# A reordered prologue, feature rows issued two a slot, and auxiliary work kept to slots 1 to 3 of every four

## The chip, the cores and the metric

The kernel runs on one core of one Trainium2 chip. The metric is the time of one execution on the device in microseconds (us), median of several runs. TensorE is called PE here, VectorE DVE, ScalarE ACT, GpSimd POOL and SyncE SP.

## What is computed

One layer on 1024 rows of 256 numbers: `x + attention(layernorm(x)) + ffn(layernorm(x))`. Attention has 16 heads of 16 numbers and two softmaxes over the same causal scores, one of them with a term from 8 "splat" features a head. The feed-forward part sends each row to the 2 best of 16 experts (at most 128 rows each) and to one shared expert.

```python
scores = einsum('bhid,bhjd->bhij', q, k) / sqrt(hd)
std_out = out_proj(softmax(where(mask, scores, neg)))
splat_attn = einsum(amp_b * qg, kg) + strength * einsum(amp_b * qg * qd, kg * kd)
gsa_out = out_proj(softmax(where(mask, scores + sensitivity * splat_attn, neg)))
attn = (1 - blend) * std_out + blend * gsa_out
...
h = silu(buf @ W1.T) * (buf @ W3.T)          # per expert, 128 rows of buf
y = sum over the 2 chosen experts of w * (h @ W2.T)
shared = (silu(xn @ Ws1.T) * (xn @ Ws3.T)) @ Ws2.T
```

## The kernel before

**Prologue.** The rows are normalized and transposed (`xnT`), and projected to q and k (`proj`). Exponentials and tanh of further products are the splat features (`feat`), `v` is projected, and the router's scores are made (`gate`). Each of these is an entry of the list `PRO`, which PE works off in order over five PSUM banks. q, k and the two feature tensors, each in two halves (eight items in `SPLIT_ORDER`), are written as three bf16 parts: `part0` and `part1` on ACT, the remainders by `rest_of` on DVE, and the third part by `third_of`, on DVE for items 0 to 3 and on POOL for items 4 to 7 (`POOL_THIRDS`). From these parts in `split`, SP's queue gathers the operand rows of each group into `stage`: 12 rows of q and k (`load_qk_row`, three buffers) and 19 of features (`load_feature_row`, two buffers). The last feature row comes from `gap_scratch`.

**Row maxima.** The softmax subtracts a row maximum, which rides as two extra rows of the q operand. The tasks `max2` and `max` make the scores of a row tile on PE and reduce them on DVE (`mx`); `max0` has the 6 tasks of the first query chunk of 512 rows, `max1` the 16 of the second. `shift` turns the result, negated and split in two, into a row (`mhl`, then `mT`), which SP writes to `stage` (`shift_rows`). In the prologue this is done for group 0, inside each group for the group after it.

**Groups.** There are 8 groups of two heads. A group walks over 6 pairs of key tiles, two pairs of the first query chunk and four of the second. One pair takes four slots, so a group has 24. On PE a pair is: the product of probabilities and v of the pair before (`pv`), slot 0, the splat scores of one key tile (`splat`), slot 1, `splat` of the other, slot 2, the plain scores of the next pair's first tile (`std`), slot 3, `std` of the second. ACT takes the exponential after each `std` and `splat`. In the slots stand auxiliary tasks by the table `PLAN`: the maxima and shifts, the output transposes `oT`, the routing steps `route` (on DVE, group 0), the shared expert in groups 0 and 1 (`sgu`, `shT`, `sy`), four experts in each of groups 2 to 5 (`xT`, `gu`, `hT`, `y`), and at the end `add`, `rows` and `out`. They share three PSUM banks in turn: a task waits on PE until DVE has emptied the bank of the third task before it (`aux_free`). For `gu` and `sgu` ACT makes a tanh behind its exponential of the same slot.

**SP's queue** walks over the same slots. At a `y` it waits until DVE has emptied it, writes it out and fetches the weights of the third expert after it; at a `shift` it waits for `mT`. One feature row of the next group is issued in each of slots 2 to 20, and one q or k row of the group after that in each of slots 0 to 11. PE waits for all 19 feature rows (`f_in`) before the first `splat` of a group.

## Time and profile before

| | us |
|---|---|
| runs | 407.89, 400.78, 406.73; median 406.73 |
| profiled execution | 399.62 |
| its span, first to last instruction | 397.8 |
| PE busy | 331.2 |
| DVE busy | 234.1 |
| ACT busy | 192.7 |

The profile is of one execution, and 1.8 us of its time lie outside the span. Busy times of the engines overlap. A group boundary is read from the copy `pv_sb<-ps` of a group's second chunk on DVE.

### The profile page before, as it was taken

The page shows a single profiled execution, that of the slowest core. Times are in us where ns is not written, and L with a number is a line of the kernel's source. Part 1 is how long each engine was busy: PE and PEld are TensorE (multiplying, and loading weights), DVE is VectorE, ACT ScalarE, POOL GpSimd, SP SyncE. Part 2 cuts the span into 40 slices and gives each one's busy share as a digit, 9 for nine tenths or more (in the row PEclk, how much of TensorE's full clock was granted, in tenths as well). Part 3 has the DMA queues.
Part 4 walks back from the last instruction along what each step waited for, and adds up shares of the span by engine and source line. Part 5 has one row for each costly group of instructions (what it writes and reads, how often), then busy time and mean ns, then how long its engine had stood idle before and what let it go on. Part 6 is the DMA issues. An engine that isn't in the chain of part 4 may idle for free.

```text
span 397.8 us, 6179 instructions
## 1 busy us (share of the span) xinstructions
PE 331.2 (83%) x2172; PEld 170.9 (43%) x2172; DVE 234.1 (59%) x613; ACT 192.7 (48%) x277; POOL 66.2 (17%) x82
## 2 busy tenths in 40 slices
PE   0999198588978999899978987999979999989974
PEld 0643075244434444444444443554535445434442
DVE  4566745768764754566446654584657646865322
ACT  1798721444534454445533553354445536857630
POOL 6200530000017630000000000010000004720000
PEclk9999777579999999999999999899999999999995
DMA  6328433050434333445543554346453333540011
GB/s 214 118 27 103 77 40 54 1 78 3 58 66 98 48 63 46 105 114 127 127 98 82 142 151 98 54 115 135 114 125 107 63 48 89 130 91 0 2 54 53
DMA packets 27330, 33.01 MB, mean 83 GB/s; under 512 B 6593, under 2 KB 20097, under 8 KB 27297
## 3 DMA queue, kind: packets, MB, share of 16 engines
q1 hardware_dynamic: 23745, 28.32, 34.1%
q0 software_dynamic: 2128, 4.22, 3.8%
q8 instruction: 19, 0.31, 0.3%
q10 hardware_dynamic: 1424, 0.04, 0.2%
q14 instruction: 14, 0.11, 0.1%
HBM read 15.60 MB, written 4.28 MB: 50 GB/s over the span
## 4 chain that ended last, share of the span: by engine, by line
PE 67%; DVE 15%; ACT 9%; DMA 4%; issue 3%; SPq 1%; DVEq 0%; ACTq 0%
PE ps L791 16%; PE ps L719 8%; PE ps L762 7%; ACT arena_p L610 6%; DVE mx L1065 6%; PE ps L692 5%; PE ps L774 5%; PE ps L728 5%; PE ps L650 3%; DMA stage<-gap_scratch 2%; PE ps L747 2%; PE ps L669 2%; PE ps L732 2%; PE ps L765 1%; PE ps L709 1%
## 5 line engine op out<-in xcount | busy, mean ns | idle before, releaser
L610 ACT ACTIVATE arena_p<-ps 128x1024 f32<-128x1024 f32 (+1 forms) x192 | 145.8, 811 | 87.8 <-PE ps L774 63.6
L1065 DVE TENSOR_REDUCE mx<-ps 128x1 f32<-128x512 f32 (+3 forms) x160 | 91.7, 591 | 60.7 <-PE ps L694 44.8
L791 PE MATMUL ps<-arena_p,v_full 128*32 128x512 f32 (+3 forms) x768 | 71.9, 492 | 0.6 <-ACT arena_p L610 0.6
L692 PE MATMUL ps<-stage 96*128 96x512 bf16 (+3 forms) x160 | 56.6, 369 | 8.3 <-DVE mx L1061 4.1
L762 PE MATMUL ps<-stage 98*128 98x512 bf16 (+1 forms) x192 | 50.9, 332 | 7.7 <-ACT arena_p L610 7.0
L774 PE MATMUL ps<-stage 98*128 98x512 bf16 (+1 forms) x192 | 46.5, 332 | 12.3 <-DMA stage<-gap_scratch 7.0
L615 ACT ACTIVATE small<-ps 128x176 f32<-128x176 f32 x24 | 7.6, 317 | 67.2 <-PE ps L719 67.2
L370 POOL DMA_INDIRECT wt<-xn_scratch,ids_sb x16 | 15.2, 949 | 146.3 <-PE ps L709 141.6
L791 PEld LDWEIGHTS ps<-arena_p,v_full 128*32 128x32 f32 x768 | 20.1, 109 | 34.3 <-issue 29.1
L692 PEld LDWEIGHTS ps<-stage 96*128 96x128 bf16 x160 | 15.6, 99 | 44.5 <-issue 24.8
L728 PE MATMUL ps<-arena_o,small 88*128 88x256 f32 x96 | 26.0, 393 | 5.4 <-DVE small L1088 5.3
L762 PEld LDWEIGHTS ps<-stage 98*128 98x128 bf16 x192 | 18.3, 99 | 27.2 <-ACT arena_p L610 15.9
L774 PEld LDWEIGHTS ps<-stage 98*128 98x128 bf16 x192 | 16.7, 98 | 28.2 <-ACT arena_p L610 8.9
L378 POOL DMA_INDIRECT ids_scratch<-tok,sidx x16 | 15.5, 966 | 68.6 <-DVE sidx L1019 64.1
L765 PE MATMUL ps<-mask_t,ident_b 128*128 128x128 bf16 x128 | 26.1, 223 | 0.0
L719 PE MATMUL ps<-w_sb,wt 128*128 128x352 f32 x64 | 23.5, 491 | 0.4
L694 PE MATMUL ps<-mask_n,ident_b 128*128 128x128 bf16 x96 | 22.3, 233 | 0.0
L728 PEld LDWEIGHTS ps<-arena_o,small 88*128 88x128 f32 x96 | 16.6, 190 | 10.4 <-DVE small L1088 8.1
L400 POOL DMA_INDIRECT xx<-ye_scratch,gidx x16 | 15.5, 968 | 32.9 <-issue 32.9
L1116 DVE COPY pv_sb<-ps 128x512 f32<-128x512 f32 x16 | 11.0, 690 | 16.1 <-PE ps L791 15.6
L1084 DVE SCALAR_TENSOR_TENSOR small<-small,ps 128x176 f32<-128x176 f32 x24 | 8.1, 338 | 21.0 <-ACT small L615 21.0
L885 DVE TENSOR_TENSOR acc<-ps,acc 128x256 f32<-128x256 f32 (+1 forms) x14 | 7.5, 538 | 17.1 <-PE ps L747 13.3
(189 smaller groups left out, 418.5 us busy)
## 6 DMA issues: line engine op xcount, KB each, us to landing
w_sb<-in_w_dram SPq DMA_DIRECT2D x16, 352.0 KB
stage<-split SPq DMA_DIRECT2D x48, 96.0 KB
stage<-split SPq DMA_DIRECT2D x48, 64.0 KB
arena_o<-in_w_dram SPq DMA_DIRECT2D x16, 176.0 KB
stage<-split SPq DMA_DIRECT2D x80, 32.0 KB
ye_scratch<-wt SPq DMA_DIRECT2D x16, 128.0 KB, 2.3
stage<-split SPq DMA_DIRECT2D x32, 48.0 KB
acc<-in_x_dram SPq DMA_DIRECT2D x2, 512.0 KB, 4.6
```

What stands on the lines that cost most here:

```text
L378: nc.gpsimd.indirect_dma_start(out=ids_d[:, :], out_offset=bass.IndirectOffsetOnAxis(ap=sidx[:, k, n:n + 1], axis=0), in_=tok[:, n:n + 1], ...
L400: nc.gpsimd.indirect_dma_start(out=gath[:, k, n, :], out_offset=None, in_=ye_d[:, :], in_offset=bass.IndirectOffsetOnAxis(ap=gidx[:, k, n: ...
L610: A(to, ps[:, 1 + 2 * s:3 + 2 * s, off:CH], ACT.Exp, scale=SCALE).then_inc(done, 1)
L692: ins = M(b[:, 0:n1 - n0], lhs, ks[0:KR, pr, h, n0:n1], start=True, stop=not diag)
L694: ins = M(b[:, n1 - n0 - P:n1 - n0], ident_b[:, :], mask_n[:, :], start=False, stop=True)
L719: ins = M(b[:, 0:2 * I], lhs, w13_sb[:, wb, k, :], start=k == 0, stop=k == KD - 1)
L728: ins = M(b[:, 0:D], hT[:, c, :], w2_sb[:, wb, c, :], start=c == 0, stop=c == 1)
L762: ins = M(b[:, off:CH], ks[:, pr, h, (jb + s) * P:(jb + s + 1) * P], qs[:, pr, h, ic * CH + off:(ic + 1) * CH], start=True, stop=not diag)
L765: ins = M(b[:, off:off + P], ident_b[:, :], mask_t[:, :], start=False, stop=True)
L774: ins = M(ps[:, 1 + 2 * s + h, off:CH], fk[:, pr, h, (jb + s) * P:(jb + s + 1) * P], fq[:, pr, h, ic * CH + off:(ic + 1) * CH], start=Fals ...
L791: ins = M(ps[c:c + 2 * HD, 0, off:CH], v_full[:, jb + s, g * GH + h, :], of, start=jb + s == 0, stop=end)
L1065: V.reduce_max(mx[:, it // TC, h, it % TC, pc:pc + 1], b[:, 0:n1 - n0], AX.X).then_inc(aux_free, 1)
```

## The change

`gate` moves ahead of `v` in the prologue, on PE and on ACT; two of the `v` products now come before the first shift and two after it. On ACT the feature evacuations and the parts of items 4 to 7 are interleaved. The third parts of items 4 and 5 move from POOL to DVE. Those of items 2 and 3 (heads 8 to 15, used from group 4 on) move from DVE to POOL, behind a new semaphore `late_thirds` that DVE signals at the start of group 0; SP waits for them in group 1. All 16 tasks of `max1` stay in the prologue (`LATER = 16`), and the second shift of the prologue moves to slot 1 of group 0, on every engine and in SP's queue. ACT runs one small Exp behind the gate's square root.

In the groups, maxima and `oT` no longer stand in slots 0, 4, 8, ...; the expert tasks are laid over two pairs at a time by a fixed table (`xT` may still stand in such a slot). In group 0 the maxima for group 1 begin at slot 5 instead of 0. The feature rows are issued two a slot from slot 0, the q and k rows in slots 10 to 21.

```diff
+        PRO += [("gate", 0)] + [("v", n) for n in range(NT // 2)]
...
-        POOL_THIRDS = (4, 5, 6, 7)
+        POOL_THIRDS = (6, 7, 2, 3)
...
-        maxima = spread(max0, 0, 5) + [(8, ("shift", 0))] + spread(max1, 6, 20) + [(22, ("shift", 1))]
-
-        def chain(tasks, each, at):
-            return [(1 + 21 * f // each + n, (k, at + f)) for f in range(each) for k, n in tasks]
+
+
+        def spread_late(tasks, first, last):
+            late = [n for n in range(first, last + 1) if n % 4]
+            return [(late[len(late) * n // len(tasks)], t) for n, t in enumerate(tasks)]
+
+        maxima = spread_late(max0, 0, 6) + [(9, ("shift", 0))] + spread_late(max1, 7, 20) + [(22, ("shift", 1))]
+        LATER = 16
+        first_rest = [(1, ("pre", ("shift", 1)))]
+        first_maxima = spread_late(max0, 5, 9) + [(12, ("shift", 0))] + spread_late(max1, 10, 20) + [(22, ("shift", 1))]
+
+        def chain(tasks, at):
+            return [(n + 12 * (f // 2), (k, at + f)) for f in range(4) for k, n in tasks[f % 2]]
+        SHARED = ((("sgu", 2), ("shT", 5), ("sy", 6)), (("sgu", 7), ("shT", 9), ("sy", 10)))
+        EXPERT = ((("xT", 0), ("gu", 2), ("hT", 5), ("y", 6)), (("xT", 5), ("gu", 7), ("hT", 9), ("y", 10)))
         PLAN = []
         for g in range(NG):
-            lists = [[(10, ("oT", 0))]]
+            lists = [[(11, ("oT", 0))]]
             if g:
-                lists.append([(2, ("oT", 1))])
+                lists.append([(3, ("oT", 1))])
+            else:
+                lists.append(first_rest)
             if g < NG - 1:
-                lists.append(maxima)
+                lists.append(maxima if g else first_maxima)
...
-                lists.append(chain((("sgu", 0), ("shT", 2), ("sy", 3)), SG, g * SG))
+                lists.append(chain(SHARED, g * SG))
             elif g < G1:
-                lists.append(chain((("xT", 0), ("gu", 1), ("hT", 3), ("y", 4)), EG, (g - G0) * EG))
+                lists.append(chain(EXPERT, (g - G0) * EG))
...
+        PRE1 = max1[0:LATER]
...
+                if at == POOL_THIRDS[2]:
+                    pool.wait_ge(late_thirds, 1)
...
-            shift_rows(-1, 1, 0)
...
-                    if g + 2 < NG and at < N_QK:
-                        load_qk_row(sp, g + 2, (g + 2) % QB, at, qk_in[(g + 2) % QB])
-                    if g + 1 < NG and 2 <= at < 2 + N_F:
-                        load_feature_row(sp, g + 1, (g + 1) % 2, at - 2, f_in[(g + 1) % 2])
+                    if g + 1 < NG:
+                        for j in range(2 * at, min(2 * at + 2, N_F)):
+                            load_feature_row(sp, g + 1, (g + 1) % 2, j, f_in[(g + 1) % 2])
+                    if g + 2 < NG and 0 <= at - 10 < N_QK:
+                        if at == 10 and g == 1:
+                            for late in (2, 3):
+                                sp.wait_ge(part_done[late], 1)
+                        load_qk_row(sp, g + 2, (g + 2) % QB, at - 10, qk_in[(g + 2) % QB])
...
+            for w in range(2):
+                evacuate(("feat", (1, 0, w)))
             part0(5)
-            for tc in range(NC):
-                for w in range(2):
-                    evacuate(("feat", (1, tc, w)))
-                part1(4 + tc)
-            for at in (6, 7):
-                part0(at)
-            for at in (6, 7):
-                part1(at)
+            part1(4)
+            for w in range(2):
+                evacuate(("feat", (1, 1, w)))
+            part0(6)
+            part1(5)
+            part0(7)
+            part1(6)
+            part1(7)
+            act.wait_ge(gate_dve, 1)
+            A(g_[2][:, :, :], g_[1][:, :, :], ACT.Exp, scale=-1.0).then_inc(gate_act, 1)
             for n in range(NT // 2):
                 evacuate(("v", n))
-            act.wait_ge(gate_dve, 1)
-            A(g_[2][:, :, :], g_[1][:, :, :], ACT.Exp, scale=-1.0).then_inc(gate_act, 1)
             act.wait_ge(gate_dve, 2)
             A(g_[4][:, :, :], g_[3][:, :, :], ACT.Ln).then_inc(gate_act, 1)
             act.wait_ge(gate_dve, 3)
             A(g_[10][:, :, :], g_[11][:, :, :], ACT.Sqrt).then_inc(gate_act, 1)
 
-            for at in range(8):
+            A(TMP, GG, ACT.Exp)
...
+            prologue(n_v + 1)
             aux(-1, ("shift", 0), 0)
-            for n in range(n_v + 1, len(PRO)):
-                prologue(n)
+            prologue(n_v + 2)
+            prologue(n_v + 3)
...
-            third_of(2)
-            third_of(3)
             product(0)
             rest_of(4)
             rest_of(5)
+            third_of(4)
             product(1)
             rest_of(6)
+            third_of(5)
             rest_of(7)
+            n = PRO.index(("gate", 0))
+            dve.wait_ge(pro_full, n + 1)
+            V.tensor_copy(G[0], ps[:, n % PB, 0:NT * E].rearrange("p (n e) -> p n e", e=E)).then_inc(pro_dve, 1)
...
-            for t in PRE0:
-                aux(-1, t)
-            for t in max1[0:8]:
+            for t in max0:
                 aux(-1, t)
             gate()
-            for t in max1[8:12]:
+            aux(-1, ("shift", 0))
+            for t in PRE1[0:4]:
                 aux(-1, t)
             plus_one()
-            for t in max1[12:]:
+            for t in PRE1[4:]:
                 aux(-1, t)
-            aux(-1, ("shift", 1))
             softplus()
 
+            V.memset(bound[:, 0:1], 0.0).then_inc(late_thirds, 1)
```

SP's queue in group 4, at the feature rows' end. `ye_scratch` is `y` (before, the fourth expert's; after, the second's), `w13_sb` and `arena_o` are weights, `stage2<-gap_scratch` is the last feature row and `stage0<-mT` a shift. Before, and then after:

```order
L308 DMA stage3<-split 32x1x1024
L308 DMA stage3<-split 16x1x1024
L483 DMA ye_scratch<-wt 128x256 [waits aux_free]
L473 DMA w13_sb<-in_w13_dram 128x2x352
L474 DMA arena_o<-in_w2_dram 88x2x256
L311 DMA stage2<-gap_scratch 2x2048
L427 DMA stage0<-mT 2x4x128 [waits aux_free]
L427 DMA stage0<-mT 2x4x128
```

```order
L322 DMA stage3<-split 16x1x1024
L444 DMA stage0<-mT 2x4x128 [waits aux_free]
L444 DMA stage0<-mT 2x4x128
L325 DMA stage2<-gap_scratch 2x2048
L501 DMA ye_scratch<-wt 128x256 [waits aux_free]
L489 DMA w13_sb<-in_w13_dram 128x2x352
L490 DMA arena_o<-in_w2_dram 88x2x256
L309 DMA stage0<-split 48x1x1024
L309 DMA stage0<-split 32x1x1024
```

The last feature row stood behind the group's last `y`; it now stands ahead of the second of four, at slot 9, and the q rows follow that `y`.

DVE in the prologue, from the rests of items 2 and 3 to those of items 6 and 7 (`split<-rest` and `split<-arena_p` are third parts, `arena_o<-` is a product of features). Before, and then after:

```order
L892 SCALAR_TENSOR_TENSOR rest<-xx,split 128x1024 [waits part_done0,first_part]
L892 SCALAR_TENSOR_TENSOR rest<-xx,split 128x1024 [waits part_done1,first_part]
L885 TENSOR_TENSOR split<-rest,split 128x1024 [waits second_part,second_rest] x2
L1122 SCALAR_TENSOR_TENSOR arena_o<-arena_o,par 128x1024 [waits pro_act]
L892 SCALAR_TENSOR_TENSOR arena_p<-arena_o,par,split 128x1024 [waits first_part]
L892 SCALAR_TENSOR_TENSOR arena_p<-arena_o,split 128x1024 [waits first_part]
L885 TENSOR_TENSOR arena_o<-arena_o 128x1024 [waits pro_act]
L892 SCALAR_TENSOR_TENSOR arena_p<-arena_o,split 128x1024 [waits first_part] x2
```

```order
L923 SCALAR_TENSOR_TENSOR rest<-xx,split 128x1024 [waits part_done0,first_part]
L923 SCALAR_TENSOR_TENSOR rest<-xx,split 128x1024 [waits part_done1,first_part]
L1150 SCALAR_TENSOR_TENSOR arena_o<-arena_o,par 128x1024 [waits pro_act]
L923 SCALAR_TENSOR_TENSOR arena_p<-arena_o,par,split 128x1024 [waits first_part]
L923 SCALAR_TENSOR_TENSOR arena_p<-arena_o,split 128x1024 [waits first_part]
L916 TENSOR_TENSOR split<-arena_p,split 128x1024 [waits second_part,second_rest]
L916 TENSOR_TENSOR arena_o<-arena_o 128x1024 [waits pro_act]
L923 SCALAR_TENSOR_TENSOR arena_p<-arena_o,split 128x1024 [waits first_part]
L916 TENSOR_TENSOR split<-arena_p,split 128x1024 [waits second_part,second_rest]
L923 SCALAR_TENSOR_TENSOR arena_p<-arena_o,split 128x1024 [waits first_part]
L1166 COPY w13_sb<-ps 128x128 [waits pro_full]
```

Two third parts left their place between the rests and the first product, two others came in among the rests of items 4 to 7, and the copy of the gate's scores stands at the end.

PE in the fourth pair of group 2 (`stage1,stage0` is a maximum and `stage0,stage1` is `std`; `stage2,stage3` is `splat`; `w13_sb,wt` is `gu`). Before, and then after:

```order
L692 MATMUL ps<-stage1,stage0 128x512 [waits aux_free,qk_in0]
L694 MATMUL ps<-mask_n,ident_b 128x128
L719 MATMUL ps<-w13_sb,wt 128x352 [waits w_in2,aux_free]
L719 MATMUL ps<-w13_sb,wt 128x352
L774 MATMUL ps<-stage2,stage3 128x512 [waits std_exp]
L774 MATMUL ps<-stage2,stage3 128x512
L692 MATMUL ps<-stage1,stage0 128x512 [waits aux_free,qk_in0]
L774 MATMUL ps<-stage2,stage3 128x512 [waits std_exp]
L774 MATMUL ps<-stage2,stage3 128x512
```

```order
L800 MATMUL ps<-stage2,stage3 128x512 [waits std_exp]
L800 MATMUL ps<-stage2,stage3 128x512
L718 MATMUL ps<-stage1,stage0 128x512 [waits aux_free,qk_in0]
L718 MATMUL ps<-stage1,stage0 128x128 [waits aux_free,qk_in0]
L720 MATMUL ps<-mask_n,ident_b 128x128
L745 MATMUL ps<-w13_sb,wt 128x352 [waits w_in2,aux_free]
L745 MATMUL ps<-w13_sb,wt 128x352
L788 MATMUL ps<-stage0,stage1 128x512 [waits gsa_exp]
L791 MATMUL ps<-mask_t,ident_b 128x128
L788 MATMUL ps<-stage0,stage1 128x512
L791 MATMUL ps<-mask_t,ident_b 128x128
L718 MATMUL ps<-stage1,stage0 128x512 [waits aux_free,qk_in0]
L718 MATMUL ps<-stage1,stage0 128x256 [waits aux_free,qk_in0]
L720 MATMUL ps<-mask_n,ident_b 128x128
L788 MATMUL ps<-stage0,stage1 128x384 [waits gsa_exp]
```

The expert product, with a maximum ahead of it in slot 12, directly preceded the first `splat` of the pair; now it stands in slot 14, ahead of `std`, with two maxima in front and two behind.

## Rows read from the trace of the kernel before

**Rows 1.** DVE, ACT and POOL timelines, prologue; in brackets idle time ahead and its end.

```profile
33.43 1.23 DVE L885 TENSOR_TENSOR split<-rest,split 128x1024 bf16<-128x1024 f32 x1 [1.05 <-ACT split L553]
...
42.82 2.17 DVE L885 TENSOR_TENSOR arena_o<-arena_o 128x1024 f32<-128x1024 f32 x1 [2.03 <-ACT arena_o L534]
44.91 4.28 DVE L892 SCALAR_TENSOR_TENSOR arena_p<-arena_o,split 128x1024 f32<-128x1024 f32 x2
...
38.48 1.06 ACT L548 ACTIVATE split<-arena_o 128x1024 bf16<-128x1024 f32 x1 [1.52 <-DVE arena_o L1122]
...
41.78 5.19 POOL L354 TENSOR_TENSOR split<-arena_p,split 128x1024 bf16<-128x1024 f32 x2 [27.14 <-ACT split L553]
```

**Rows 2.** PE timeline, prologue (L684, L692 maxima; L669 v; L643 gate).

```profile
44.22 0.23 PE L684 MATMUL ps<-stage 96*128 96x128 bf16 x1 [4.82 <-issue]
...
49.77 0.61 PE L692 MATMUL ps<-stage 96*128 96x512 bf16 x1 [4.13 <-DVE mx L1061]
...
51.27 3.68 PE L669 MATMUL ps<-wt,xx 128*128 128x256 f32 x8
...
55.04 5.45 PE L669 MATMUL ps<-wt,xx 128*128 128x256 f32 x24
60.32 3.64 PE L643 MATMUL ps<-gw_sb,xx 128*128 128x16 f32 x32
```

**Rows 3.** DVE and ACT timelines, from the second chunk's maxima to the first exponential.

```profile
64.22 4.07 DVE L1065 TENSOR_REDUCE mx<-ps 128x1 f32<-128x512 f32 x8 [8.87 <-PE ps L692]
...
78.20 1.28 ACT L610 ACT_TABLE_LOAD   x1
79.49 1.73 ACT L610 ACTIVATE arena_p<-ps 128x1024 f32<-128x1024 f32 x2
```

**Rows 4.** Waits of PE in the whole span: us in total, times, longest.

```profile
PE ps L697 <- DVE mhl L885: 8.0, 8, 1.8
PE ps L762 <- ACT arena_p L610: 7.0, 15, 0.8
PE ps L774 <- DMA stage<-gap_scratch: 7.0, 3, 2.4
PE ps L728 <- DVE small L1088: 5.3, 9, 2.2
PE ps L774 <- ACT arena_p L610: 5.2, 8, 1.3
```

**Rows 5.** SP's queue and PE at the change from group 2 to group 3.

```profile
201.81 0.35 SPq L483 DMA_DIRECT2D ye_scratch<-wt  x1
...
203.38 0.27 SPq L311 DMA_DIRECT2D stage<-gap_scratch  x1
...
206.42 0.61 PE L774 MATMUL ps<-stage 98*128 98x512 bf16 x2 [2.27 <-DMA stage<-gap_scratch]
```

**Rows 6.** DVE timeline: the evacuation that ends each of groups 1 to 4.

```profile
164.47 0.69 DVE L1116 COPY pv_sb<-ps 128x512 f32<-128x512 f32 x1 [1.71 <-PE ps L791]
...
203.84 0.69 DVE L1116 COPY pv_sb<-ps 128x512 f32<-128x512 f32 x1 [1.77 <-PE ps L791]
...
245.60 0.69 DVE L1116 COPY pv_sb<-ps 128x512 f32<-128x512 f32 x1 [1.77 <-PE ps L791]
...
289.34 0.69 DVE L1116 COPY pv_sb<-ps 128x512 f32<-128x512 f32 x1 [1.77 <-PE ps L791]
```

**Rows 7.** Windows: length, busy us (instructions) of PE, PEld, DVE, ACT, POOL, PEclk, DMA share, GB/s.

```profile
44.20:54.80 10.60, 6.45 (x24) 3.84 (x24) 9.61 (x14) 3.64 (x4) 6.97 (x3) 0.52 0.26 32
...
65.00:85.50 20.50, 14.00 (x47) 5.56 (x47) 15.17 (x44) 7.31 (x10) 0.00 (x0) 0.50 0.23 37
...
249.20:252.80 3.60, 3.60 (x13) 2.48 (x12) 2.56 (x8) 0.73 (x1) 0.94 (x1) 0.53 0.69 117
...
206.50:245.60 39.10, 36.17 (x257) 18.72 (x258) 22.95 (x60) 18.70 (x28) 3.78 (x4) 1.00 0.48 111
```

**Rows 8.** PE timeline in group 3: a matmul behind an expert matmul.

```profile
229.53 0.61 PE L774 MATMUL ps<-stage 98*128 98x512 bf16 x2 [0.67 <-ACT arena_p L610]
```

23 lines of the change are left out of this document (15 added, 8 removed).

## The prediction

> **What bounds the kernel now.** I read the windows first. Over a whole group without disturbance PE is busy 36.17 of 39.10 us at full clock, against 22.95 on DVE and 18.70 on ACT [rows 7]. So PE sets the pace of the groups, and the change, which takes no work from PE, can only take away its waits. The table of waits says what they are: 8.0 us for the second step of a shift (`mhl`), 7.0 and 5.2 for exponentials on ACT, 7.0 in three waits for the last feature row (`gap_scratch`), 5.3 for the transposed expert rows in `small` [rows 4]. Group by group, the evacuations stand 39.37, 41.76 and 43.74 us apart [rows 6]. The first distance has no feature wait; the second has one; the third has one and 3.6 us at 0.53 of the clock right behind it [rows 7]. The prologue is another matter: there PE sits idle for 4.82 and 4.13 us, DVE and ACT hand work to each other, and the first exponential starts at 79.49 [rows 2, 3]. What brings that start forward shortens everything behind it.
>
> **Prologue: 5.8 us off.** Step by step:
>
> - *gate.* Its 32 matmuls take 3.64 us, between the last `v` and the maxima of the second chunk [rows 2]. Before those maxima PE idles 4.82 us, because the feature evacuations on ACT are not done and then a branch is taken. gate now fills that idle time. Gain 3.6. The branch now follows gate, and there are 4.82 - 3.64 = 1.2 us for it; if it needs more, up to 1 of the gain is lost.
> - *DVE ahead of the first maxima.* DVE is what PE waits 4.13 us for [rows 2]. Product and two rests there take 2.17 and 4.28 us, while POOL makes third parts for 5.19 us; the same shape of operation takes 1.23 elsewhere [rows 1]. With items 4 and 5 off POOL they should take 3 x 1.23 = 3.7, a gain of 2.8. Two thirds and the copy of gate's scores come in, 2 x 1.23 + 0.3 (estimate for an eighth of the columns) = 2.8. What stays is that the features are ready sooner: two thirds no longer stand ahead of the first product, and ACT no longer idles 1.52 us for it [rows 1]. I take 1.4 (bounds 0 and 2.8).
> - *From the second chunk's maxima to the exponential.* This takes 79.49 - 64.22 = 15.3 us; eight of the sixteen reductions are 4.07 of it [rows 3]. They all stay. The other 15.3 - 8.1 = 7.2 are the router's steps, the shift and the table load. gate's copy and two small operations leave it, and the second shift no longer stands between the last maximum and the router's last step. I estimate 0.8 of the 7.2. The early Exp saves nothing: the table load of 1.28 us still follows the square root, which still waits for DVE [rows 3].
> - *Clock.* The 8 matmuls of the first `v` take 3.68 us at half clock, the other 24 take 5.45 [rows 2]. The granted clock was 0.52 from 44.2 to 54.8, behind idle PE [rows 7]. All four `v` at half clock would be 14.7 us, all at full clock 4 x 1.82 = 7.3; now they are 9.1, and I leave it there (bounds +5.6, -1.8).
>
> Sum: 3.6 + 1.4 + 0.8 = 5.8, bounds -2.2 and 9.0.
>
> The Trainium skill, "TensorE: Matmul & The Clock Gate", section "HAM oscillation — how this bites in real kernels", says that idle stretches bring the half clock back and steady work ends it. By that rule gate in the idle stretch would keep the clock up through `v` and the prologue would gain 1.8 us more, 7.6; the trace agrees that the half clock came behind idle time.
>
> **Feature rows: 7.0 us off, and 2.0 of clock.** In groups 2 to 4 SP reaches the last feature row only after it has waited for the group's last `y` (201.81) and fetched weights; it issues the row at 203.38, and PE goes on at 206.42 after 2.27 us idle [rows 5]. A slot lasts 39.10 / 24 = 1.6 us [rows 7]. After, this row stands at slot 9, fifteen slots or 24 us before its use, with the `y` of slot 6 and the shift of slot 9 ahead of it. The three waits go: 7.0 [rows 4]. The stretch at half clock stood behind the second of them, so its cost goes too: 43.74 - 41.76 = 2.0 [rows 6]. Behind the changed order wait the q and k rows: the last four are issued after the `y` of slot 18. They are needed at slot 1 of the next group, seven slots or 11 us later, against the 3.0 us from issue to use seen above. I cost them at nothing; as a rival below they cost what the feature row cost. The bursts (up to 12 short rows at once) meet a DMA share of 0.48 [rows 7], so weights and gathers, needed several slots later, should not be late.
>
> **Slots 1 to 3: 4.5 us off.** Behind slot 0 stands a `splat` that waits for ACT's exponential of a `std`, but the 16 matmuls of `pv` have already covered it. Slots 1 to 3 cover the other three, and there more work means less waiting. The waits for ACT total 12.2 us [rows 4]; without the table load (1.28) and an eighth of the rest for the last group, whose table hardly changes, that is 9.5. `gu` makes most of them: its tanh stands ahead of an exponential, as at 229.53 (0.67) [rows 8]. With the `gu` at slots 2, 7, 14 and 19 I walked one group: some 0.15 is left at slot 3, 0.35 at slot 8, which is now empty, 0.45 at slot 15, nothing at 19. Together 0.95 a group, 6.6 in seven; with waits so short that two of these three may vanish I put what is left at 5.5, a gain of 4. The last maximum moves from slot 20 to 19, two slots and an expert product ahead of the shift, so of 8.0 us for `mhl` [rows 4] some 5 go, besides the prologue's 1.8. Against that: `y` follows `hT` by one slot everywhere, with two DVE reductions of 0.51 [rows 3] between, and the wait for `small` grows from 5.3 [rows 4] by about 3; and group 0 gets its 22 maxima in 15 slots beside the routing, +1.5. Net 4 + 5 - 3 - 1.5 = 4.5 (bounds -9 and +10, the latter the rival of the banks).
>
> *Late third parts.* Two POOL operations of 5.19 / 2 = 2.6 us [rows 1] now run at the start of group 0. DVE has the second shift's copy and six small routing operations then, and PE needs nothing of DVE before slot 5, except that copy. Cost nothing, bound +4.
>
> The Trainium skill, "SBUF — State Buffer", section "SBUF: two separate sides", says that GpSimd and a DVE operation with two inputs in SBUF exclude each other for a whole instruction. By that rule each of two routing operations may stand still for 2.6 us and the sum would be up to 4 us worse; the trace agrees on the stretched operations of the prologue.
>
> **The sum.** 5.8 + 7.0 + 2.0 + 4.5 = 19.3 us. The profiled execution took 399.62, so 380.3. That execution was faster than all three runs (400.78 to 407.89), 7.1 below the median. In it one of three feature waits was followed by half clock for 2.0 us; if all three were in other runs, 4 of the 7.1 come from there and go with the waits. I add 2 of the other 3 and predict **382**. Its own range is 374 (`mhl` and ACT waits all gone, `v` at full clock) to 390.
>
> **Rivals.**
>
> 1. *The q and k rows come late* and take the place of the feature row at slot 1. For: they now wait behind three `y`. Against: the 11 us above. Price: the 7.0 and the 2.0 come back, 391.
> 2. *Half clock through all of `v`* and into group 0, where slots 0 to 4 are thinner than now; from 65.0 to 85.5 the clock was 0.50 [rows 7]. Price 5.6, 388. Against: less idle time ahead of `v`.
> 3. *Banks, in part.* A DVE reduction takes 0.51 us, its matmul about 0.25. Seven slots of a group now hold two maxima or more (ten in group 0), and a third task waits for the bank of the first. If a fifth of the 52 pairs cost PE both reductions: 52 x 1.02 / 5 = 10.6, 392.
> 4. *Banks in full, slower than before.* The same mechanism in all groups: 53 us if every pair pays. It undoes the 19.3 when more than 36% do; at 60% it is 32, 414. Against: DVE is busy 22.95 of 39.10 [rows 7], and between the pairs stand `splat`, `std` and `gu`.
> 5. *The feature rows don't come sooner.* SP's queue may be so full that the row is still behind the last `y`. Against: slot 9 is ahead of it in the list. 391.
> 6. *Full clock through `v`*, because gate leaves PE less idle ahead of it: 1.8 us less, 380. Against: 1.2 us or more of idle time stay there, and DVE's first maxima still keep PE waiting.
> 7. *POOL stops DVE at the start of group 0*, two routing operations for 2.6 us each. It decides if the second shift's copy stands behind them: 4 us more, 386.
>
> **How the numbers follow.** Chances: forecast 0.48, rivals 1 to 7: 0.08, 0.08, 0.10, 0.05, 0.05, 0.12, 0.04. The range 373 to 394 takes in the forecast's own range and all rivals but 4, and leaves out what lies below. A measurement of this kernel tells about 2%, here 8 us, so faster by over 2% means below 398.6: the forecast, rivals 1, 2, 5, 6, 7 and nearly all of 3, less a little for what I have not thought of, 0.90; the same 0.06; slower 0.04.
>
> **What the profile after would show.** First exponential near 73.7 (prologue). gate's matmuls right behind the last feature matmuls, and DVE's first maximum near 47.7. No wait of PE for `gap_scratch`, and none for another row of `stage` at slot 1. Group distances of 38.3 to 39.2 in groups 2 to 5, all alike, with no half clock there. Waits for `mhl` under 2 us in all; those for ACT near 8; those for `small` above 7. If instead PE waits for `mx` for more than 5 us, the banks (rivals 3 and 4) were underrated. Wrong altogether would be the forecast if groups got longer than 39.4, or the first exponential came no sooner than 78.

## Result, and the profile after

| | before | after |
|---|---|---|
| runs | 407.31 us median of 4 (400.78 to 410.28) | 381.46 us median of 4 (377.05 to 382.43) |
| profiled execution, its span | 399.62, 397.8 | 382.43, 380.6 |
| PE, DVE, ACT busy | 331.2, 234.1, 192.7 | 336.6, 230.5, 194.0 |

The ratio is 0.943, 95% interval [0.926, 0.960]: faster, and at the forecast time. Ratios here and below are taken from undisturbed executions alone, so they are not always the quotient of the medians shown. The total was right. Within it one part was credited to the wrong edit, and group 0 cost more than three times what was forecast, as the profile and the experiments show. The two profiled executions lie at opposite ends of their kernels: that of before is faster than all of its four runs, that of after is the slowest of its four. So 17.2 us lie between the two spans and 25.9 between the two medians.

The page after, its first lines (span; busy us, share, instructions):

```profile
span 380.6 us, 6180 instructions
PE 336.6 (88%) x2172; PEld 174.8 (46%) x2172; DVE 230.5 (61%) x614; ACT 194.0 (51%) x278; POOL 65.6 (17%) x82
```

The waits of PE after, whole span (us in total, times, longest), answering to [rows 4]:

```profile
...
PE ps L754 <- DVE small L1116: 6.3, 9, 2.2
PE ps L718 <- DVE mx L1093: 4.6, 9, 2.8
PE ps L788 <- ACT arena_p L636: 4.4, 11, 0.8
PE ps L800 <- ACT arena_p L636: 3.9, 2, 3.6
PE ps L754 <- DVE mT L1107: 2.0, 6, 0.3
PE ps L718 <- DVE mx L1089: 1.7, 2, 1.5
...
PE ps L723 <- DVE mhl L916: 0.4, 1, 0.4
```

`gap_scratch` is gone, `mhl` fell from 8.0 to 0.4, and ACT from 12.2 to 8.3, of which 3.6 is the wait ahead of the very first `splat`, 1.3 before. What grew is `small` and its neighbour `mT`, 5.3 to 8.3 together.

The evacuations that end groups 0 to 3, answering to [rows 6] (DVE timeline):

```profile
124.14 0.69 DVE L1144 COPY pv_sb<-ps 128x512 f32<-128x512 f32 x1 [1.46 <-PE ps L817]
...
161.34 0.69 DVE L1144 COPY pv_sb<-ps 128x512 f32<-128x512 f32 x1 [1.46 <-PE ps L817]
...
199.44 0.69 DVE L1144 COPY pv_sb<-ps 128x512 f32<-128x512 f32 x1 [1.39 <-PE ps L817]
...
237.61 0.69 DVE L1144 COPY pv_sb<-ps 128x512 f32<-128x512 f32 x1 [1.39 <-PE ps L817]
```

In the same way all stages were read, in us (a group from evacuation to evacuation, group 0 from the first exponential):

| | to first exponential | group 0 | 1 | 2 | 3 | 4 | 5 | 6 | 7 |
|---|---|---|---|---|---|---|---|---|---|
| before | 79.49 | 45.62 | 39.36 | 39.37 | 41.76 | 43.74 | 41.91 | 27.33 | 27.50 |
| after | 72.98 | 51.16 | 37.20 | 38.10 | 38.17 | 38.75 | 38.16 | 26.52 | 27.58 |
| difference | -6.5 | +5.5 | -2.2 | -1.3 | -3.6 | -5.0 | -3.8 | -0.8 | +0.1 |

With +0.3 behind the last evacuation this makes the 17.2 us between the two spans. The middle groups and the prologue gave what was forecast or more; group 0 took back nearly all that the prologue gave.

The prologue after, PE timeline (gate L669, `v` L695), answering to [rows 2]:

```profile
40.23 4.50 PE L669 MATMUL ps<-gw_sb,xx 128*128 128x16 f32 x32
44.56 0.27 PE L710 MATMUL ps<-stage 96*128 96x128 bf16 x1
...
47.67 0.61 PE L718 MATMUL ps<-stage 96*128 96x512 bf16 x1 [1.45 <-DVE mx L1089]
...
49.17 5.69 PE L695 MATMUL ps<-wt,xx 128*128 128x256 f32 x16
...
54.95 3.72 PE L695 MATMUL ps<-wt,xx 128*128 128x256 f32 x16
58.50 0.44 PE L718 MATMUL ps<-stage 96*128 96x512 bf16 x2
...
74.13 1.01 PE L800 MATMUL ps<-stage 98*128 98x512 bf16 x2 [3.61 <-ACT arena_p L636]
```

gate fills the old idle time, and the first maximum starts at 44.56 where it started at 44.22; the wait for DVE is 1.45 instead of 4.13; `v` takes 9.4 instead of 9.1. Most of its first half still runs at half clock: 5.69 us for 16 matmuls, where the other 16 take 3.72. So do the first two stretches in these windows (length, busy us (instructions) of PE, PEld, DVE, ACT, POOL, PEclk, DMA share, GB/s), both in group 0; the third is the undisturbed group that answers to [rows 7]:

```profile
73.50:84.00 10.50, 9.40 (x38) 3.82 (x39) 3.31 (x12) 4.21 (x8) 2.02 (x1) 0.51 0.18 24
111.00:118.00 7.00, 6.13 (x18) 3.77 (x19) 4.23 (x12) 0.00 (x0) 4.52 (x5) 0.52 0.59 169
206.50:245.00 38.50, 36.98 (x263) 19.33 (x261) 24.49 (x64) 19.62 (x29) 3.78 (x4) 1.00 0.57 126
```

Group 0 as a whole, from the first exponential to its evacuation, before and then after:

```profile
79.49:125.11 45.62, 37.70 (x253) 18.71 (x254) 30.51 (x101) 20.38 (x30) 5.88 (x6) 0.93 0.32 59
```

```profile
72.98:124.14 51.16, 43.27 (x256) 21.10 (x257) 30.66 (x103) 20.53 (x31) 11.68 (x12) 0.83 0.29 51
```

PE is idle for 7.9 us in both. The whole 5.5 us by which the group got longer is busy time of PE, for nearly the same instructions at a mean clock of 0.83 instead of 0.93.

### The profile page after: what moved, and what is told of

The parts are those of the page before. It is cut to its first block, busy times and chain, and to the rows that moved or that the text cites. A ratio compares the mean times of both kernels' runs of the same rounds, so it can differ in the third digit from the quotient of the medians.

```text
span 380.6 us, 6180 instructions
## 1 busy us (share of the span) xinstructions
PE 336.6 (88%) x2172; PEld 174.8 (46%) x2172; DVE 230.5 (61%) x614; ACT 194.0 (51%) x278; POOL 65.6 (17%) x82
## 4 chain that ended last, share of the span: by engine, by line
PE 72%; DVE 13%; ACT 9%; issue 4%; DMA 1%; DVEq 0%; SPq 0%; ACTq 0%
PE ps L817 16%; PE ps L745 9%; PE ps L800 8%; PE ps L788 7%; PE ps L754 7%; PE ps L718 6%; ACT arena_p L636 6%; DVE mx L1093 5%; PE ps L676 4%; PE ps L773 2%; PE ps L695 2%; PE ps L791 2%; ACT small L641 1%; PE ps L758 1%; DMA acc<-in_x_dram 1%
## 5 line engine op out<-in xcount | busy, mean ns | idle before, releaser
L1093 DVE TENSOR_REDUCE mx<-ps 128x1 f32<-128x512 f32 (+3 forms) x160 | 88.9, 590 | 29.7 <-PE ps L718 19.5
L817 PE MATMUL ps<-arena_p,v_full 128*32 128x512 f32 (+3 forms) x768 | 73.4, 500 | 0.6 <-ACT arena_p L636 0.6
L718 PE MATMUL ps<-stage 96*128 96x512 bf16 (+3 forms) x160 | 51.6, 362 | 7.5 <-DVE mx L1093 4.6
L788 PE MATMUL ps<-stage 98*128 98x512 bf16 (+1 forms) x192 | 51.9, 337 | 5.0 <-ACT arena_p L636 4.4
L800 PE MATMUL ps<-stage 98*128 98x512 bf16 (+1 forms) x192 | 47.6, 333 | 4.5 <-ACT arena_p L636 3.9
L754 PE MATMUL ps<-arena_o,small 88*128 88x256 f32 x96 | 27.5, 410 | 8.3 <-DVE small L1116 6.3
L788 PEld LDWEIGHTS ps<-stage 98*128 98x128 bf16 x192 | 19.0, 101 | 23.8 <-ACT arena_p L636 10.7
L800 PEld LDWEIGHTS ps<-stage 98*128 98x128 bf16 x192 | 14.8, 98 | 29.7 <-issue 14.0
L754 PEld LDWEIGHTS ps<-arena_o,small 88*128 88x128 f32 x96 | 16.8, 195 | 14.4 <-DVE small L1116 9.7
L745 PE MATMUL ps<-w_sb,wt 128*128 128x352 f32 x64 | 23.0, 482 | 0.1
L395 POOL DMA_INDIRECT ids_scratch<-tok,sidx x16 | 15.5, 966 | 41.3 <-DVE sidx L1047 36.7
L1144 DVE COPY pv_sb<-ps 128x512 f32<-128x512 f32 x16 | 11.1, 691 | 14.4 <-PE ps L817 13.7
```

What stands on the lines that cost most here:

```text
L395: nc.gpsimd.indirect_dma_start(out=ids_d[:, :], out_offset=bass.IndirectOffsetOnAxis(ap=sidx[:, k, n:n + 1], axis=0), in_=tok[:, n:n + 1], ...
L718: ins = M(b[:, 0:n1 - n0], lhs, ks[0:KR, pr, h, n0:n1], start=True, stop=not diag)
L745: ins = M(b[:, 0:2 * I], lhs, w13_sb[:, wb, k, :], start=k == 0, stop=k == KD - 1)
L754: ins = M(b[:, 0:D], hT[:, c, :], w2_sb[:, wb, c, :], start=c == 0, stop=c == 1)
L788: ins = M(b[:, off:CH], ks[:, pr, h, (jb + s) * P:(jb + s + 1) * P], qs[:, pr, h, ic * CH + off:(ic + 1) * CH], start=True, stop=not diag)
L800: ins = M(ps[:, 1 + 2 * s + h, off:CH], fk[:, pr, h, (jb + s) * P:(jb + s + 1) * P], fq[:, pr, h, ic * CH + off:(ic + 1) * CH], start=Fals ...
```

## Experiments: the parts alone

Four runs on one chip, where the kernel before took 407.01 us (median of 18).

**Feature rows alone (e1_rows).** The kernel before with the changed kernel's order of rows:

```diff
-                    if g + 2 < NG and at < N_QK:
-                        load_qk_row(sp, g + 2, (g + 2) % QB, at, qk_in[(g + 2) % QB])
-                    if g + 1 < NG and 2 <= at < 2 + N_F:
-                        load_feature_row(sp, g + 1, (g + 1) % 2, at - 2, f_in[(g + 1) % 2])
+                    if g + 1 < NG:
+                        for j in range(2 * at, min(2 * at + 2, N_F)):
+                            load_feature_row(sp, g + 1, (g + 1) % 2, j, f_in[(g + 1) % 2])
+                    if g + 2 < NG and 0 <= at - 10 < N_QK:
+                        load_qk_row(sp, g + 2, (g + 2) % QB, at - 10, qk_in[(g + 2) % QB])
```

> The kernel before with one part of the change: feature rows two a slot from slot 0, q and k rows in slots 10 to 21. Theory A (the parts add up, as the sum has it): the three waits of PE for gap_scratch and the stretch at half clock behind one of them go, 9 us off, about 398. Rival B (the feature rows matter only where the groups are short of other waits): the wait for gap_scratch goes, but waits for mhl and ACT grow behind it, 2 to 4 us off, about 404. Rival C (the q and k rows come late in this longer table): no gain, 407. A and B are told apart by the distances of the evacuations of groups 2 to 4: 39.4 in A, over 40.5 in B.

Measured: 413.19 us, ratio 1.027 [1.018, 1.035]. All three theories missed; it is slower, and whether by more than 2% the interval leaves open. The `gap_scratch` waits are gone, and another took their place. SP's queue and PE at the change from group 3 to group 4:

```profile
247.19 0.34 SPq L483 DMA_DIRECT2D ye_scratch<-wt  x1
247.57 0.43 SPq L473 DMA_DIRECT2D w_sb<-in_w_dram  x1
248.05 0.44 SPq L474 DMA_DIRECT2D arena_o<-in_w_dram  x1
248.53 1.21 SPq L295 DMA_DIRECT2D stage<-split  x2
```

```profile
252.34 0.23 PE L685 MATMUL ps<-stage 96*128 96x128 bf16 x1 [3.19 <-DMA stage<-split]
```

```profile
PE ps L685 <- DMA stage<-split: 11.6, 4, 4.3
```

The last q and k rows are issued at 248.53, behind the `y` of slot 20 and its weight fetches, and the old table has maxima that need them in slot 0 of the next group. Four such waits are 11.6 us, more than the 7.0 that they replace. This is rival 1 of the prediction, real and dearer than priced, but only under the old slot table.

**Slot table alone (e2_slots).** The kernel before with `spread_late`, `SHARED`, `EXPERT` and the new places of `oT`; group 0 gets the general `maxima`:

```diff
-        maxima = spread(max0, 0, 5) + [(8, ("shift", 0))] + spread(max1, 6, 20) + [(22, ("shift", 1))]
+        maxima = spread_late(max0, 0, 6) + [(9, ("shift", 0))] + spread_late(max1, 7, 20) + [(22, ("shift", 1))]
...
-                lists.append(chain((("xT", 0), ("gu", 1), ("hT", 3), ("y", 4)), EG, (g - G0) * EG))
+                lists.append(chain(EXPERT, (g - G0) * EG))
```

> The kernel before with one part of the change: the new slot table for maxima, oT, shared expert and experts; in group 0 the maxima start at slot 1, since the prologue is the old one. Theory A (the table gains about 1 us a group in groups 1 to 5 and loses in group 0): 4.5 us off, about 402, with gap_scratch waits still there. Rival B (the table is worth more than the sum said: groups 1 and 2 went from 39.36 to 37.20 and 38.10 in the changed kernel although the feature rows never held group 1 up): 8 us off, about 399. Rival C (the table costs in group 0 what it gains later): 407. The distance of group 1 tells: 37.2 to 37.5 in B, 38.3 in A.

Measured: 387.20 us, ratio 0.961 [0.954, 0.968]. Groups 1 to 5 took 37.20, 38.09, 38.17, 38.74 and 38.15 us: to 0.01 us those of the whole change. Group 0 took 49.11. No wait for `gap_scratch` is left, though the rows keep their old order. Rival B pointed the right way and was still too small.

**Prologue alone (e3_prologue).** The changed kernel with the old table and the old order of rows:

```diff
-                lists.append(maxima if g else first_maxima)
+                lists.append(maxima)
...
-                lists.append(chain(EXPERT, (g - G0) * EG))
+                lists.append(chain((("xT", 0), ("gu", 1), ("hT", 3), ("y", 4)), EG, (g - G0) * EG))
```

> The kernel before with the prologue of the changed kernel alone (gate ahead of v, third parts exchanged, second shift in slot 1 of group 0, early Exp); slot table and order of SP's rows are the old ones. Theory A (additive): first exponential near 73.0 instead of 79.5, group 0 no longer than before (45.6 from the first exponential to its evacuation), 6 us off, about 401. Rival B (group 0 pays, since the routing and the second shift now meet it and the half clock comes in it): group 0 takes 48 or more, 2 to 3 us off, about 404.

Measured: 398.76 us, ratio 0.993 [0.989, 0.996]. The first exponential came at 71.05, 8.4 us sooner than before, but group 0 took 49.16, 3.5 more than before, with PE busy for 41.44 us instead of 37.70. Groups 1 to 4 together took 4.3 more, with mean clocks of 0.96, 0.98, 0.96 and 0.96 in them, where before had 1.00 in groups 1 to 3. Rival B as to group 0, by the clock. The span of this profile, 398.8, is no shorter than that of before, but it is of the slowest of 12 runs (396.13 to 400.60) and that of before of a fast one, so what the groups behind lost here is not shown to come from the edit.

**Old order of rows (e4_oldrows).** The changed kernel with the `-` lines of the first diff in place of its `+` lines, and SP's wait for the late thirds at slot 0 of group 1.

> The changed kernel with the old order of SP's rows (q and k rows in slots 0 to 11, one feature row a slot in 2 to 20). Theory A: the wait for gap_scratch comes back in groups 2 to 4 at 2.3 us each, with one stretch of half clock, so 7 to 9 us more than the changed kernel, 389 to 391. Rival B (in the new table the group's last y stands at slot 22 as before but groups are shorter, so the row comes even later against its use): 10 us or more, over 392. Rival C (the rows no longer matter): 382.

Measured: 379.10 us (376.63 to 382.25), ratio 0.942 [0.931, 0.952], against 0.943 for the change. Rival C: in the changed kernel the new order of the rows is worth nothing. Groups 1 to 5 agree to 0.01 us again. SP's queue at the end of group 2 says why:

```profile
190.31 0.42 SPq L325 DMA_DIRECT2D stage<-gap_scratch  x1
191.91 1.37 SPq L444 DMA_DIRECT2D stage<-mT  x2
193.50 0.36 SPq L501 DMA_DIRECT2D ye_scratch<-wt  x1
```

The last feature row still stands at slot 20. It is the `y` that moved, from slot 20, ahead of this row, to slot 22, behind it: compare [rows 5].

## Experiments: what in the table does it

Four runs on a second chip, where the kernel before took 437.27 us (median of 7) and groups 0 and 6 of every profile were 10 to 20 us longer (last section). Groups 2 to 5 can be compared across chips; of the total only the ratio to before on the same chip. Group 1 can't: it took 40.01 and 40.16 us in the first two of these runs, whose slot table is that of before, where it took 39.36.

**One slot sooner (e5_feat1).**

```diff
-                    if g + 1 < NG and 2 <= at < 2 + N_F:
-                        load_feature_row(sp, g + 1, (g + 1) % 2, at - 2, f_in[(g + 1) % 2])
+                    if g + 1 < NG and 1 <= at < 1 + N_F:
+                        load_feature_row(sp, g + 1, (g + 1) % 2, at - 1, f_in[(g + 1) % 2])
```

> The kernel before with each feature row one slot sooner (slots 1 to 19 instead of 2 to 20), so that the last one is issued ahead of the y of slot 20 and not behind it; nothing else. Theory A (the wait for gap_scratch is a matter of which side of the last y the row stands on, and the changed kernel's new slot table removed it by moving that y to slot 22): no gap_scratch wait, groups 2 to 4 at about 39.4, 8 to 9 us less than before in the profiled execution, span near 389. Rival B (SP's queue is late as a whole, one slot is not enough): waits of 1 us or more stay, span near 394. Rival C (other waits take their place): span over 395.

Measured: ratio 0.969 [0.966, 0.973]. The evacuations of groups 2 to 4:

```profile
220.21 0.69 DVE L1116 COPY pv_sb<-ps 128x512 f32<-128x512 f32 x1 [1.77 <-PE ps L791]
...
259.58 0.69 DVE L1116 COPY pv_sb<-ps 128x512 f32<-128x512 f32 x1 [1.77 <-PE ps L791]
...
299.24 0.69 DVE L1116 COPY pv_sb<-ps 128x512 f32<-128x512 f32 x1 [1.77 <-PE ps L791]
```

Groups 2 to 5 take 39.37, 39.37, 39.66 and 39.37 us, 157.8 together against 166.8 before: 9.0 us. That is theory A's size, and the 7.0 + 2.0 of the prediction, by the one profile of before that there is, with one stretch at half clock in it. On this chip the whole kernel fell by 13.7 us; where the other 4.7 lie is open, as before was not profiled here. The span itself was off by what the second chip adds.

**q and k rows two slots sooner (e6_rows8).** The first experiment with `at - 8` for `at - 10`.

> The kernel of the rows-alone run with the q and k rows in slots 8 to 19 instead of 10 to 21, all ahead of the y of slot 20. Theory A (that run lost because its last q and k rows stood behind the y of slot 20 and the first maxima of the next group wait for them in slot 0): the wait for stage rows at the maxima goes, and with the gap_scratch wait gone too the time is that of the one-slot-sooner run, span near 389. Rival B (two rows a slot are slower to land as such): waits for stage rows stay, span over 395.

Measured: ratio 0.972 [0.969, 0.976]; groups 2 to 5 take 39.36, 39.36, 39.66 and 39.36. Theory A: two rows a slot do no harm as such. What decides is on which side of a `y` the last row of each kind stands.

**Maxima alone (e7_maxima).** Only the `maxima` line of the second diff.

> The kernel before with only the maxima and first shift of the new slot table (no maximum in slots 0, 4, 8 and so on; first shift at 9; last maximum at 19 instead of 20); experts, shared expert and oT stay. Theory A: the mhl waits (8.0 us) go to about 1, gap_scratch waits stay, 6 to 7 us less, span near 391. Rival B (maxima crowd beside gu and y and wait for banks): mhl gone, but mx or ACT waits grow by as much, span 395 or more.

Measured: ratio 1.009 [1.006, 1.011], slower. Group 1, without experts, took 38.39, less than the 40.01 and 40.16 of the two runs above, but groups 2 to 5 took 40.43, 43.10, 45.25 and 43.90, 5.9 us more than before. Waits for `mhl` fell to 2.2 in all and none is in these groups; `gap_scratch` kept 6.8. Rival B's sign, but not its account: in group 2 the waits for ACT are 2.2 against 2.0 before, those for `mx` 0.2, and one of 0.6 without a releaser is new, while PE's busy time went from 36.45 to 37.10 at full clock. Group 5 had a mean clock of 0.96, where before had 1.00, so a part of its 2.0 is the clock's. What slowed PE in the other groups stays open.

**Chains alone (e8_chains).** Only the expert, shared expert and `oT` lines of it.

> The kernel before with only the expert, shared expert and oT places of the new slot table (last y at slot 22); the maxima stay. Theory A (this half takes the last y behind the last feature row): no gap_scratch wait and no half clock in group 3, but mhl waits stay at 7 to 8; ACT waits down from 12 to about 8; small waits up 2; group 0 longer by 2 to 3 because of the wider chain beside the routing: 9 us less, span near 389. Rival B: most of the 13 us that the whole table gave in the profile come from the maxima, and this half gives under 5, span over 393.

Measured: ratio 0.964 [0.961, 0.967]. Groups 2 to 5 take 39.11, 39.11, 39.56 and 39.10, 156.9 together, 9.9 us less than before. Theory A. PE's waits in groups 1 to 5 have no `gap_scratch`, and `mhl` even more than before (5.7 against 3.2). The first line is the wait ahead of group 1's first `splat`, at the end of the stretch that this chip lengthens:

```profile
PE ps L775 <- ACT arena_p L611: 8.8, 1, 8.8
PE ps L698 <- DVE mhl L886: 5.7, 5, 1.1
PE ps L729 <- DVE small L1089: 2.5, 7, 0.7
PE ps L693 <- DVE small L1089: 2.3, 4, 0.6
PE ps L763 <- ACT arena_p L611: 2.2, 4, 0.6
```

The two halves do not add. In groups 2 to 5 the maxima cost 5.9 us under the old chains; under the new ones they gain 156.9 - 153.2 = 3.7.

## Experiments: group 0

Four runs of variants of the changed kernel on a third chip, with 437.53 us for the kernel before (median of 7). The change's own ratio, 0.943, is from a chip on which the kernel before takes 407 us, with an interval of 0.017 to each side, so of these totals only large differences count. The third chip too lengthens groups 0 and 6, from about 118 us on; what comes before that in group 0 can be read.

**Maxima of group 0 from slot 1 (e9_g0max).**

```diff
-                lists.append(maxima if g else first_maxima)
+                lists.append(maxima)
```

> The changed kernel with the maxima of group 0 placed as in the other groups (slots 1 to 6 and 7 to 19) instead of from slot 5 on. Theory A (group 0 got longer because PE has nothing but the pairs in slots 0 to 4 and 22 maxima are packed into the rest): the wait of 3.6 us before the first splat is partly filled, group 0 takes 2 us less, about 379.5. Rival B (the first slots wait for ACT and the table load whatever stands in them, and DVE has the routing and the second shift there): no change within 1 us, 381.5.

Measured: 413.36 us, ratio 0.944 [0.938, 0.949]. The wait before the first `splat` is 3.65 us, against 3.61: rival B as to that wait. It also costs group 0 nothing new: that `splat` starts 1.15 us behind the first exponential, from which group 0 is counted, and started 1.17 behind it in the kernel before. The `pv` behind slot 19, at 118.25 in the changed kernel, started at 115.55, 2.7 us sooner, with a half clock stretch that was also shorter there, so theory A is not refuted for the rest of the group.

**Routing behind the shared expert (e10_route).**

```diff
-            if g == 0:
-                lists.append(spread([("route", k) for k in range(ROUTE)], 1, 22))
             if g < G0:
                 lists.append(chain(SHARED, g * SG))
+                if g == 0:
+                    lists.append(spread([("route", k) for k in range(ROUTE)], 1, 22))
```

> The changed kernel with the routing steps of group 0 placed behind, not ahead of, the shared expert's tasks of the same slot. Only DVE's order changes, in slots 10 and 17. Theory A (PE's wait of 2.2 us for small in slot 18 comes from the routing step ahead of the copy of slot 17, and starts the half clock from 111 to 118 us): that wait goes to under 0.6 us, no half clock there, group 0 takes 4 to 5 us less (47), about 377. Rival B (the wait goes but the half clock comes at another place of group 0): 2 us less, 379.5.

Measured: 411.72 us, ratio 0.938 [0.931, 0.945]. PE there, first in the changed kernel (`sy` is L754, `sgu` L745), then here:

```profile
105.43 1.92 PE L817 MATMUL ps<-arena_p,v_full 128*32 128x512 f32 x16
...
111.87 2.05 PE L754 MATMUL ps<-arena_o,small 88*128 88x256 f32 x4 [2.17 <-DVE small L1116]
...
115.31 2.66 PE L745 MATMUL ps<-w_sb,xx 128*128 128x352 f32 x4
```

```profile
104.02 1.92 PE L817 MATMUL ps<-arena_p,v_full 128*32 128x512 f32 x16
...
108.23 1.10 PE L754 MATMUL ps<-arena_o,small 88*128 88x256 f32 x4
...
111.05 1.05 PE L718 MATMUL ps<-stage 96*128 96x512 bf16 x2 [1.39 <-DVE mx L1093]
...
112.00 2.66 PE L745 MATMUL ps<-w_sb,xx 128*128 128x352 f32 x4
```

The wait of 2.17 us for `small` is gone, but one of 1.39 for a maximum has come behind it: from `pv` to `sgu` it is 8.0 us instead of 9.9. The half clock stays, now behind that other wait, since the `sgu` takes 2.66 at either place. Theory A as to the wait for `small`, rival B as to the clock; what the half clock does without any wait there this run doesn't show. Whether the whole kernel is faster than the change these totals don't tell.

The same wait need not bring the half clock either. In the run with the old order of rows PE waits the same 2.17 us for the same copy, and goes on at full clock. The kernel before has such a wait of 2.17 us too, at 117.61, with four of the same matmuls in 1.10 us behind it; with the slot table alone and the prologue alone the wait is 2.18 and these matmuls take 2.05, at half clock. The run with the old order of rows:

```profile
110.36 1.10 PE L753 MATMUL ps<-arena_o,small 88*128 88x256 f32 x4 [2.17 <-DVE small L1115]
...
112.13 1.40 PE L744 MATMUL ps<-w_sb,xx 128*128 128x352 f32 x4
```

That profile has 47.94 us for group 0 where the changed kernel's has 51.16. PE is idle for 7.9 us of it, as in the changed kernel, so the 3.2 us between them stand with the clock. The other 2.3 are no full clock figure: from 91 to 97 the mean clock of this run was 0.72 too.

**`y` and `sy` one slot later (e11_y7), and with it the routing (e12_both).**

```diff
-        EXPERT = ((("xT", 0), ("gu", 2), ("hT", 5), ("y", 6)), (("xT", 5), ("gu", 7), ("hT", 9), ("y", 10)))
+        EXPERT = ((("xT", 0), ("gu", 2), ("hT", 5), ("y", 7)), (("xT", 5), ("gu", 7), ("hT", 9), ("y", 11)))
```

(`SHARED` alike.)

> The changed kernel with y and sy one slot later, two slots behind hT and shT instead of one. Theory A (the waits for small, 6.3 us, and for mT at y, 2.0 us, come from the copy that DVE makes between hT and y): both go to under 1 us in all, groups 1 to 5 get 0.5 to 1 us shorter each, the wait in slot 18 of group 0 goes too; 6 us less, about 375.5. Rival B (y now stands beside a maximum and waits for its bank instead, and the last y stands behind the shift in slot 23): small and mT gone, mx or aux waits up by as much, within 2 us of 381.5.

> The changed kernel with both edits: y and sy one slot later, and the routing steps behind the shared expert's tasks of the same slot. Theory A (if the later y already covers the routing step): the same as with the later y alone. Rival B (the routing step takes longer than the slot that y was moved by): 1 to 3 us less than with the later y alone, all of it in group 0.

Measured: 416.76 us, ratio 0.950 [0.944, 0.957], and 417.84 us, 0.955 [0.949, 0.962]. Both are slower than the other two on this chip. Groups 2 to 5 take 38.49, 38.56, 39.23 and 38.55 us, 1.7 in all more than in the change. PE's waits in groups 1 to 5:

```profile
PE ps L788 <- ACT arena_p L636: 3.5, 10, 0.4
PE ps L754 <- DVE onv L916: 2.9, 5, 0.6
PE ps L718 <- DVE mx L1093: 0.8, 4, 0.2
```

The change has 1.9 for `small`, 1.7 for `mT` and 1.5 for ACT there. Theory A is refuted for the middle groups: the 3.6 us of waits for `small` and `mT` became 2.9 behind another DVE operation (`onv`), and ACT's grew by 2.0. That `y` in its new slot makes PE later for the scores that ACT needs next is my reading and was not tried by itself. Rival B had the result but named the wrong wait. With the later `y`, the routing makes no difference in the middle groups, as both theories have it, and total and group 0 (64.79 against 64.69) show no gain: rival B of the last run falls, in a group 0 that the chip itself disturbs.

## Why the prediction was right, and where it was not

- **Total.** 382.0 forecast, 381.46 measured. By the sum: 19.3 us off forecast, 17.2 between the two spans.
- **Prologue**, forecast -5.8, measured -6.5. gate's place gave 3.3 of the 3.6: its matmuls started at 40.23, where the idle time that they fill had begun at 39.4, and took 4.50 instead of 3.64 since the clock fell during them; the branch behind them left no gap. The wait for DVE's first maxima fell by 2.7, and from the first maximum to `v` it is 2.4 us less, where the term had 1.4; DVE ran the same shapes in 1.22 each. `v` took 0.3 more. The rest of the way gave 15.3 - 14.1 = 1.2 instead of 0.8. `v` stayed partly at half clock: gate in the idle stretch did not keep the clock up. PE had worked without a gap since 29.75 when the clock went from 1.00 to 0.50 at about 43.0, in the middle of gate's matmuls. The Trainium skill, "TensorE: Matmul & The Clock Gate", section "HAM oscillation — how this bites in real kernels", has idle stretches bring the half clock back and steady work end it; by that rule rival 6 would have come. This execution disagrees as to the first half of that, since no idle time stood ahead of the fall; as to the second it agrees, as the other 16 matmuls of `v` ran at full clock. The same prologue in the runs with the old table and with the old order of rows took gate in 3.75 us, at a clock of 0.97 and 1.00 from 40 to 44; there PE idled for 2.90 us soon behind it, the clock was 0.59 and 0.57 from 44 to 52, and `v` took 8.7 and 8.9 us, where 7.3 would have been full clock. So rival 6 came in none of them. Their first exponentials, at 71.05 and 71.64, show that the prologue's gain moves by 2 us between executions.
- **Feature rows and clock, 7.0 + 2.0.** The size was right, as e5_feat1 measures it by itself (9.0 in groups 2 to 5). The step that failed is the cause: "After, this row stands at slot 9" is true but decides nothing. The part of the change that does it is the slot table, which moves the last `y` from slot 20 to 22, past the row of slot 20. The prediction worked out the new order of SP's queue with both parts in place and gave the first one the credit. Alone, that part costs 2.7%.
- **q and k rows late (rival 1).** Did not happen in the change, because the last `y` stands at slot 22, behind the rows of slots 10 to 21, and no maximum stands in slot 0. Without the table it happens at once, at up to 4.3 us a group.
- **Slots 1 to 3**, forecast -4.5 net with -6 in the groups behind group 0 and +1.5 in group 0. The groups behind gave some -7.5 (-16.5 less the 9.0), and group 0 cost +5.5. `mhl` went from 8.0 to 0.4, 7.6 off where the 5 and the prologue's 1.8 had been forecast. `small` and `mT` grew by 3.0, as forecast. ACT came to 8.3 against "near 8", but partly by luck: in groups 1 to 5 its waits fell from 8.2 to 1.5, by more than the 4 forecast for seven groups, and the one ahead of the first `splat` grew by 2.3, which no term had.
- **Group 0** is the term that was mis-sized, +5.5 for +1.5, and its way was another than forecast. The term was for 22 maxima in 15 slots beside the routing, that is, for waits. PE's idle time in the group is 7.9 us before and after; what grew is its busy time, by 5.6 us. In the two windows of after at 0.51 and 0.52 of the clock PE is busy for 15.5 us; before it has one stretch at half clock in the group, with 4.8 us of busy time from 79.5 to 85.5. My estimate from these: 10.7 us more at half clock, half of which, 5.3, full clock would save. Rival 2 had named half clock into group 0, for the thin slots 0 to 4. Of the 5.5, 3.2 differ from one execution to another, as the run with the old order of rows shows. The rest is not so easily put down to chance: the two profiles with the old table and the old prologue have 45.6 us there (before and e1_rows), and the four with the new table, the new prologue or both (the change, e2_slots, e3_prologue, e4_oldrows) have 47.9 to 51.2. Which wait, if any, brings the half clock there stays open.
- **Banks (rivals 3 and 4).** PE's waits for `mx` are 6.3 us, above the mark of 5 that was set for them, but 4.2 of these are two waits in the prologue (1.45 at 47.67 and 2.78 at 63.96), ahead of the groups; in groups 1 to 5 they are 0.8. So no rival here, and the mark should have left out the prologue.
- **Late third parts**, forecast 0: POOL makes them from 71.32 to 75.52, at no cost, as forecast. But DVE was idle then, waiting 4.17 us for PE's transpose of the second shift, and its routing began at 75.52. So the cost was nothing because the two never met; rival 7, and the rule that it drew on, were not put to the test.
- **Group distances** of 38.10 to 38.75 in groups 2 to 5, all at full clock; forecast 38.3 to 39.2, so three of the four were a little shorter than that.
- **Luck.** The total owes something to it. The prologue gave 0.7 us and the groups behind group 0 gave 1.5 more than forecast, group 0 cost 4.0 more, and 0.3 came in behind the last evacuation: 17.2 instead of 19.3. The 2 us that were added for the typical run rested on feature waits that are now and then followed by half clock, which no run here tests.

## What to carry to other kernels

In a queue that works in order, a late transfer is a question of what blocking entry stands ahead of it. Moving either of the two repairs it, so when a change moves both, undo one at a time before giving either the credit. A table of slots is not a sum of its rows: the maxima cost 5.9 us with the old chains and gained 3.7 with the new. Time that is gained ahead of a stage can be given back in it without a single new wait: here 5.5 of 6.5 us in group 0, where PE's idle time stayed at 7.9 us and its mean clock went from 0.93 to 0.83. So compare busy time and clock of a stage, and not its waits alone.
